# Rotary halves exchanged by ScalarE, and smaller array tiles, in the second attention of a two-layer fp32 kernel

## What is computed

```python
kv_c = kv @ W_kvc                                  # 64 compressed channels, 64 keys per batch in the kernel
q_c = q @ W_dq                                     # 96
q_nope = (q_c @ W_uq).reshape(b, lq, 16, 128);  q_rope = _rope((q_c @ W_qr).reshape(b, lq, 16, 64), lq)
k_nope, v = (kv_c @ W_uk), (kv_c @ W_uv)           # 16 heads of 128
k_rope = _rope(kv_c @ W_kr, lk)
scores = (q_nope . k_nope + q_rope . k_rope) * scale;  scores = where(good, scores, NEG)
out = softmax(scores) . v;  return out @ W_o
# _rope: x1, x2 = halves of 32;  [x1 * cos - x2 * sin, x1 * sin + x2 * cos]
# FFN: gate = silu(W_gate x), up = W_up x (704 hidden channels);  W_down (gate * up)
```

## Time and profile before

| what | us |
|---|---|
| median of 3 executions | 863.61 (861.70 to 863.77) |
| profiled execution | 862.67 |
| its span, first to last instruction | 860.87 |
| TensorE, weight loads, VectorE busy | 810.3, 692.9, 661.2 |
| ScalarE, GpSimd busy | 521.0, 457.1 |
| granted TensorE clock, mean | 0.984 |

### The profile page before, as it was taken

The page is one execution under the profiler, slowest core; times in us unless marked ns, Lnnn a source line. Parts: engine busy times, 40 slices in busy tenths (PEclk is TensorE's granted clock), DMA queues, the critical chain, the costliest instruction groups (busy, mean ns, idle before and its releaser), DMA issues.

```text
span 860.9 us, 14397 instructions
## 1 busy us (share of the span) xinstructions
PE 810.3 (94%) x4888; PEld 692.9 (80%) x4888; DVE 661.2 (77%) x1584; ACT 521.0 (61%) x1202; POOL 457.1 (53%) x776
## 2 busy tenths in 40 slices
PE   3777999999999999999899999999999999999998
PEld 2566888888888888888788788988888878777887
DVE  7988888899888998879988894955544758876534
ACT  6888877788678886788764645433322334646332
POOL 2485869779685996858953864252010028760000
PEclk9779999999999999999999999999999999999999
DMA  7000120012101030000100416947310000100001
GB/s 236 14 1 1 38 74 1 2 38 61 51 1 32 7 111 1 2 1 22 47 25 14 148 38 181 232 138 270 105 52 23 11 34 25 50 1 1 0 2 49
DMA packets 28376, 45.99 MB, mean 53 GB/s; under 512 B 3952, under 2 KB 18096, under 8 KB 28176
## 3 DMA queue, kind: packets, MB, share of 16 engines
q1 hardware_dynamic: 26800, 41.31, 16.4%
q10 hardware_dynamic: 1504, 3.77, 1.2%
HBM read 43.89 MB, written 1.18 MB: 52 GB/s over the span
## 4 chain that ended last, share of the span: by engine, by line
PE 66%; DVE 21%; ACT 9%; issue 3%; DMA 1%; SPq 0%; ACTq 0%; DVEq 0%
PE PS L760 18%; PE PS L829 8%; PE PS L716 5%; PE PS L621 5%; PE PS L652 4%; PE PS L690 4%; PE PS L930 3%; DVE cat L1498 3%; PE PS L885 2%; PE PS L662 2%; PE PS L643 2%; DVE yb L1494 2%; PE PS L673 2%; PE PS L920 2%; PE PS L700 2%
## 5 line engine op out<-in xcount | busy, mean ns | idle before, releaser
L2166 POOL TENSOR_SCALAR raw<-raw,mvq,rsq 128x128 f32<-128x128 f32 x312 | 187.6, 615 | 7.2 <-DVE mvq L1639 5.7
L760 PE MATMUL PS<-xq,WH 128*128 128x512 f32 x480 | 151.0, 396 | 0.0
L760 PEld LDWEIGHTS PS<-xq,WH 128*128 128x128 f32 x480 | 87.8, 190 | 17.0 <-issue 0.8
L760 PE MATMUL PS<-xq,WL 128*128 128x512 f32 x240 | 94.1, 392 | 0.0
L621 PE MATMUL PS<-WH,xq 128*128 128x256 f32 (+1 forms) x256 | 89.6, 367 | 3.6 <-issue 1.5
L621 PE MATMUL PS<-WL,xq 128*128 128x256 f32 (+1 forms) x256 | 84.9, 349 | 0.0
L1086 ACT ACTIVATE P<-PS,sm 128x256 f32<-128x256 f32 x128 | 60.7, 492 | 31.1 <-DVE sm L1667 30.9
L1592 DVE BATCH_NORM_STATS2 st<-raw 128x6 f32<-128x128 f32 x320 | 71.9, 276 | 0.9 <-ACT raw L1058 0.9
L829 PE MATMUL PS<-xq,m_hh 128*128 128x256 f32 x384 | 69.3, 281 | 1.4 <-DVE m_hl L1956 0.6
L716 PE MATMUL PS<-PH,cat 128*128 128x256 f32 x256 | 64.7, 292 | 6.2 <-DVE cat L1498 5.9
L690 PE MATMUL PS<-PT,vr 128*128 128x256 f32 x256 | 66.2, 381 | 1.0 <-ACT PT L972 1.0
(11 more groups left out here) (299 smaller groups left out, 2208.7 us busy)
## 6 DMA issues: line engine op xcount, KB each, us to landing
wst<-in_wgu SPq DMA_DIRECT2D x24, 256.0 KB, 3.7
l_KM<-share SPq DMA_DIRECT2D x16, 384.0 KB, 4.0
wst<-in_wall SPq DMA_DIRECT2D x18, 256.0 KB, 3.1
l_KM<-share SPq DMA_DIRECT2D x16, 256.0 KB, 4.8
dst<-in_wdn SPq DMA_DIRECT2D x24, 128.0 KB, 3.6
wst<-in_wkvx SPq DMA_DIRECT2D x8, 256.0 KB, 3.4
l_KM<-share SPq DMA_DIRECT2D x16, 128.0 KB, 4.1
m_pre<-in_wo ACTq DMA_DIRECT2D x1, 2048.0 KB, 10.1
```

Of the source, the lines that this page charges most:

```text
L760: t = e.matmul(PS[:, b, :], W[wi][:, gu, k, :], a[:, k, cols], start=(n == 0), stop=(n == 5))
L2166: t = e.tensor_scalar(v, v, mvq[:, par, n, 0:1], rsq[:, par, n:n + 1], ALU.add, ALU.mult)
```

## The change

It does the following:
- The exchanged copy of the rotary weights (wrt), its DMA and its matmuls go. One bank now holds two pairs of heads (a unit u; 4 units a batch). The columns of W_qr are reordered so that the first halves of two heads lie in partitions 0 to 63 and the second halves in 64 to 127. ScalarE copies the bank's upper half, negated, to the lower half of tqs and its lower half to the upper (`swap_q`); VectorE multiplies tqs by sin and the bank by cos; GpSimd adds. Two buffers of each go round.
- Queries come before scores in each n, and queries(1, 0) before the loop; each n from 0 to 4 has one part.
- `values2` is 8 matmuls of K = 64, M = 64 on the four quarters of the array, two fillings (of the four) at a time; BDK holds the keys on both halves in both column halves, with no zeros. `outmix` takes the heads in matching order.
- `absorb` fills both column halves, AT lies on 128 partitions, KA holds the compressed keys on both halves, and `keymix` alternates between the upper and the lower row half of the array.
- In the FFN, block 5 puts 64 channels of gate and 64 of up into one weight: one bank instead of two, and `f_down` there reads 64 rows.

```diff
-QUERIES = {0: (2, 3), 1: (4,), 2: (5,), 3: (6,), 4: (7,)}
+QUERIES = {0: (3,), 1: (4,), 2: (5,), 3: (6,), 4: (7,)}
-        if a == 0:
-            for part in range(2):
-                do("queries", 0, part)
+        for part in ((0, 0), (0, 1)) if a == 0 else ((1, 0),):
+            do("queries", *part)
     for n in range(11):
+        for m in QUERIES.get(n, ()):
+            do("queries", m // 2, m % 2)
         if n < 8:
             do("scores", n)
         if n % 2 and n > 2:
             do("values", (n - 3) // 2)
-        for m in QUERIES.get(n, ()):
-            do("queries", m // 2, m % 2)
...
-            "queries": lambda bb, part: [("qr", bb, p) for p in range(4 * part, 4 * part + 4)],
+            "queries": lambda bb, part: [("qr", bb, u) for u in range(2 * part, 2 * part + 2)],
...
 def keys():
                 for k in range(2):
-                    t = e.matmul(PS[0:64, b, 0:256], wkvc[:, k, :], ctxT[:, k, :], start=(k == 0), stop=(k == 1))
+                    for o in (0, 64):
+                        t = e.matmul(PS[o:o + 64, b, 0:256], wkvc[:, k, :], ctxT[:, k, :], start=(k == 0), stop=(k == 1))
 def absorb(z):
                 for h in range(4 * z, 4 * z + 4):
-                    t = e.matmul(PS[0:64, b, h % 4 * 96:h % 4 * 96 + 96], wuk[:, h, :], wuq[:, h, :], start=True, stop=True)
+                    o, i = 64 * (h % 2), h % 4 // 2 * 96
+                    t = e.matmul(PS[o:o + 64, b, i:i + 96], wuk[:, h, :], wuq[:, h, :], start=True, stop=True)
 def keymix():
-                for z in range(8):
-                    b = fill(("km", z))
-                    emptied(("aw", z // 2))
-                    for h in (2 * z, 2 * z + 1):
-                        t = e.matmul(PS[0:96, b, h % 2 * 256:h % 2 * 256 + 256], AT[:, h, :], KA[0:64, :], start=True, stop=True)
-                    t.then_inc(full[b], 1)
+                for y in range(4):
+                    banks = [fill(("km", 2 * y + o)) for o in range(2)]
+                    emptied(("aw", y))
+                    for i in range(2):
+                        for o, b in enumerate(banks):
+                            rows = slice(64 * o, 64 * o + 64)
+                            t = e.matmul(PS[0:96, b, i * 256:(i + 1) * 256], AT[rows, 2 * y + i, :], KA[rows, :],
+                                         start=True, stop=True)
+                            if i:
+                                t.then_inc(full[b], 1)
 def queries(bb, part):
-                for p in range(4 * part, 4 * part + 4):
-                    b = fill(("qr", bb, p))
-                    for z, W in enumerate((wqr, wrt)):
-                        t = e.matmul(PS[:, b, z * 256:(z + 1) * 256], W[:, p * 128:(p + 1) * 128],
+                for u in range(2 * part, 2 * part + 2):
+                    b = fill(("qr", bb, u))
+                    for i in range(2):
+                        p = 2 * u + i
+                        t = e.matmul(PS[:, b, i * 256:(i + 1) * 256], wqr[:, p * 128:(p + 1) * 128],
                                      qcT[:, bb * 256:(bb + 1) * 256], start=True, stop=True)
 def values2(bb):
-                for z in range(4):
-                    b = fill(("lv", bb, z))
-                    e.matmul(PS[:, b, :], BDK[:, bb, :], PT1[:, 2 * z:2 * z + 2, :].rearrange("p a b -> p (a b)"),
-                             start=True, stop=True).then_inc(full[b], 1)
+                for z in (0, 2):
+                    banks = [fill(("lv", bb, z + i)) for i in range(2)]
+                    for r, c, i in ((0, 0, 0), (64, 64, 0), (0, 64, 1), (64, 0, 1)):
+                        t = e.matmul(PS[c:c + 64, banks[i], :], BDK[r:r + 64, bb, c:c + 64],
+                                     PT1[r:r + 64, 2 * (z + i):2 * (z + i) + 2, :].rearrange("p a b -> p (a b)"),
+                                     start=True, stop=True)
+                        if r:
+                            t.then_inc(full[banks[i]], 1)
 def place_keys():
-                for o in (0, 64):
-                    copy(KZ[o:o + 64, :, o // 64, :], k23[o:o + 64]).then_inc(keys_in, 1)
+                for o in range(0, 128, 32):
+                    copy(KZ[o:o + 32, :, o // 32 % 2, :], k23[o:o + 32]).then_inc(keys_in, 1)
+            def swap_q(bb, part):
+                for u in range(2 * part, 2 * part + 2):
+                    n = 4 * bb + u
+                    b = w.filled(("qr", bb, u))
+                    if n > 1:
+                        w.wait_ge(added.sem, added.at[(n - 2) // 4, (n - 2) % 4])
+                    e.activation(tqs[u % 2][0:64, :], PS[64:128, b, :], ACT.Copy, scale=-1.0)
+                    copy(tqs[u % 2][64:128, :], PS[0:64, b, :]).then_inc(swapped.sem, 1)
 for a in (0, 2):   # ScalarE
                 take_qc(a)
                 take_qc(a + 1)
+                for part in ((0, 0), (0, 1)) if a == 0 else ((1, 0),):
+                    swap_q(*part)
             for n in range(11):   # ScalarE
+                for m in QUERIES.get(n, ()):
+                    swap_q(m // 2, m % 2)
                 if n % 2 and n > 2:
                     take_lv((n - 3) // 2)
                 if n < 8:
                     exps2(n)
 def gate_f(n):   # ScalarE; VectorE waits for gated_5 and multiplies rows 64:128 of the same bank
+                if j == 5:
+                    e.activation(fsg[n % 3][0:64, :], PS[0:64, b, :], ACT.Silu, scale=fsc[0:64, 5:6]).then_inc(gated_5.sem, 1)
+                    return
 def turn_q(bb, part):   # VectorE
-                    e.tensor_tensor(tq[n % 3], PS[:, b, :], tb_[:, 0:512], ALU.mult).then_inc(free[b], 1)
+                    if n > 1:
+                        w.wait_ge(added.sem, added.at[(n - 2) // 4, (n - 2) % 4])
+                    w.wait_ge(swapped.sem, swapped.at[bb, u])
+                    e.tensor_tensor(two[1], two[1], sin, ALU.mult)
+                    e.tensor_tensor(two[0], q, cos, ALU.mult).then_inc(free[b], 1)
 def add_q(bb, part):   # GpSimd
-                    e.tensor_tensor(QR[bb % 2][:, p, :], tq[n % 3][:, 0:256], tq[n % 3][:, 256:512],
+                    e.tensor_tensor(QR[bb % 2][:, 2 * u:2 * u + 2, :].rearrange("p a b -> p (a b)"), tqc[n % 2], tqs[n % 2],
                                     ALU.add).then_inc(added.sem, 1)
```

102 lines of the change are left out of this document (58 added, 44 removed).

## The result

The changed kernel took 872.45 us in the median of 8 runs (867.47 to 874.99), the kernel before 863.69 (860.54 to 865.45) beside it: ratio 1.0098, 95% interval 1.0068 to 1.0127. The forecast was 859.3, range 855.0 to 863.5: wrong in sign and outside the range. The profiled execution took 869.8 us, with a span of 868.0 against 860.87.

A forecast was written before the change was run, and what follows sets the result against it. TensorE was taken as the bound, balanced in the loop by a VectorE and ScalarE ring. Terms -1.1, +0.5, +0.9, 0, -1.5, -1.4, -0.75 gave -3.35 us on 862.67: 859.3 us, range 855 to 863.5.

The forecast's parts named there:

- TensorE loses 3.5 us per chunk and has room: Loop: fewer query matmuls take 3.5 us per chunk off TensorE; the pitch was not expected to follow.
- the ring's: Loop: VectorE and ScalarE set the pitch, 9.8 us between starts of soft(n)'s row maxima (M_n); M_0 to M_7 unchanged.
- GpSimd's sums stand ahead of the weights of that n: Loop: GpSimd adds the rotary products before converting that n's weights; VectorE and ScalarE keep the 9.8 us pitch.
- The wait at n = 3: Chunk 3's exponentials wait 4.7 us more for values(0)'s banks and copies; M_3 to M_4 takes 14.7 us.
- The opening: From keymix to the first row maximum: two-buffer ring of swap, products and GpSimd sum; maximum at 710.4 us, +0.9.
- Rival D: Opening: GpSimd's 512-column additions could take 2.2 us beside VectorE; first maximum 2 us later, 861.3 us; chance 0.15.
- Before the late stage: Ahead of keymix: absorbing keys in pairs -1.1 us, placing rotary keys with four copies +0.5 us, the rest nothing.
- Keymix: Two row tiles take 3.7 us instead of 7.14; copies through four banks let x2T copies start 2.35 us earlier.
- Tail: After the loop: values(3) -1.5 us, FFN block j = 5 at h = 0 -1.4, last down group -0.75.
- A: Values: array tiles run only in program order, 3.9 us a call; total 862.0 us; chance 0.12.
- C: Values: four tiles run one after another, 6.9 us a call; total 871.9 us; chance 0.05.
- B: Chunk 3: the new wait does not bind or is short, M_4 4.7 us earlier; total 854.6 us; chance 0.1.

The follow-up runs named there:

- e1: Changed kernel with idle matmuls into an unused bank ahead of compress(2), the queries of n = 0 to 3 and inside values(0): 868.12 us, ratio 1.0051.
- e15: The kernel of e9 with idle matmuls ahead of compress(2), queries(2, 1) and (3, 0), and inside values(0): 863.58 us, ratio 0.9986.
- e9: Changed kernel with values(0)'s copies behind chunk 3's exponentials, three rotary buffers, and GpSimd's last three weight pieces held until xn_f(0): 866.54 us, ratio 1.0049.
- e12: The kernel of e9 with TensorE's order back to scores, values, queries, and GpSimd's weight conversions behind the scaling of soft(n): 867.38 us, ratio 1.0040.
- e13: Kernel before with all edits but the rotary one, GpSimd's conversions behind the scaling, last three pieces held: 857.10 us, ratio 0.9926; run again 858.37, 0.9946.
- e16: The kernel of e15 with GpSimd's weight conversions behind the scaling of soft(n): 859.75 us, ratio 0.9956.
- e4: Changed kernel with GpSimd holding the last three FFN weight pieces (6, 7, 8) until add_l(0) is done: 868.84 us, ratio 1.0066.
- e5: Changed kernel with ScalarE's copies of values(0) put behind chunk 3's exponentials instead of ahead: 869.85 us, ratio 1.0090.
- e14: Changed kernel without ScalarE's exchange across partitions, sine products reading the bank directly, queries not rotated rightly: 865.08 us, ratio 1.0015.

## Why the prediction was wrong, point by point

**"TensorE is full in nearly all of it, at a granted clock of 1.00, which leaves the clock out of this case."** This is the step that failed first. A clock that is full because the engine is full says nothing of a change that takes work off this engine. With "TensorE loses 3.5 us per chunk and has room" I wrote down the idle time and priced it at nothing. The runs: 872.45 to 868.12 for filling the gaps (e1), and 1.0049 to 0.9986 where the other waits were mended (e15 against e9). It is not the largest term. Of the 10.5 us between the forecast and the profiled execution, by the points below, about 3.9 are matmuls at half clock, 4.4 VectorE's operations beside GpSimd's, 1.0 the start, 0.6 the late copies of l_x2T and 0.6 the tail.

**"So the pitches from M_0, M_1, M_2 and M_4 are the ring's: 9.8 each."** They were 10.4, 12.2, 10.8 and 9.9. Of the 4.0 us over the forecast from M_0 to M_3, 0.6 a chunk, 1.8, is the scaling, 2.3 us long where it was 1.65 to 1.7: GpSimd's conversions stand beside it. The forecast took 9.8 from a row that already had part of the stretch in it; without GpSimd beside it the pitch is 9.3 (e12, e13, e16). The other 2.2 is queries and scores at half clock: with the fillers of e1 all three are 10.4, and they are near it, too, in e4's execution, where hardly more than the queries ran slow.

**"GpSimd's sums stand ahead of the weights of that n"**: right, but what it delays was not followed up. The last three pieces now lie on add_l(0), whose steps of 0.16 us take 1.1 beside them. M_5 to M_7 took 23.6 and not 21.0 us: 2.6 of the 6.7. In e4 these two pitches are 20.6 together; M_4 to M_5 takes 1.2 of the gain back.

**The wait at n = 3: right in place and size, wrong in what it is worth.** M_3 to M_4 took 14.8 us, the forecast was 14.7 (the 3.4 us that it gives for TensorE at n = 4 should be 3.6, 13.4 less 9.8; no term hangs on it). But taking it away on ScalarE's side (e5) gave 1.5 us and no ratio that differs. TensorE's own chain through the same bank is only 1.5 us shorter. No order that I tried brought this pitch under 12.9 with the rotary edit.

**The opening: mechanism right, size off.** Forecast +0.9, measured +3.1. Rival D's cause, a slower sum (1.44 us in the mean and not 1.27), and exchanges of 1.22 us a unit, where 1.1 was taken, delay the copies of l_x2T by 0.6 us, counted from the start of keymix. The larger part, 1.7, is the clock again: compress(2, 3) 3.27 instead of 1.94, the sixteen query records behind it 4.01 instead of 3.6. Three buffers and the clock kept bring the opening to 25.1 (e9, e15); without the exchange, in the same order, it is 22.5 (e14).

**Before the late stage.** absorb gave 0.65 us for two calls, 1.3 in all (forecast 1.1); place_keys took 1.72 us for 0.84, +0.9 (forecast +0.5, bound +0.85). The start of keymix is 0.4 us later and not 0.6 earlier; since variants of the changed kernel that are the same up to there start keymix anywhere from 684.34 to 689.54, no run here can settle this.

**Keymix: right.** From keymix's start to the copies of x2T 5.4 us, forecast 5.5; the second half of it waited 0.39 us for a copy, as the bank argument said.

**Tail: right, but for the FFN.** values(3) gave 1.5, as forecast; block 5 for h = 0 gives 1.0 where 1.4 was forecast; the last down group begins 0.7 us sooner after f_front(5, 1) than before (4.36 to 3.65; forecast 0.75), TensorE waiting 0.81 us for Silu, product and copy as foreseen, but its 18 records then take 2.58 us and not 2.39. The rows show one cause for both: where matmuls of 64 rows follow such of 128, or the other way round, the next record starts some 0.1 us late and the first pair lasts 0.1 longer, 0.2 a change, with two changes at h = 0 and one at the end. The forecast had counted 0.2 for such changes in values and left them out here.

**The rivals.** A and C are refuted by a values call of 1.95 us; the one of 3.51 is not their case but the clock's. B, that the wait at n = 3 doesn't bind, is false in the rows and nearly true in worth. C's time, 871.9, was near the result, for a reason that had nothing to do with it: the slower side had a chance of 0.12 and no rival with the cause that decided. The one that was missing is TensorE at half clock in the idle time that the change itself makes.

**A rule that was weighed.** The values rows show 16 records of 512 columns in 1.95 us, four at a time. By the rule of strict order in the Trainium skill (TensorE: Matmul & The Clock Gate, Part 3), read so that the second pass of each fp32 matmul holds up the next tile, a call would have taken 3.9 us, an estimate from these rows. The trace does not agree with that reading.

## What to carry to other kernels

Work taken off the busiest engine does not only leave it idle: ask what its granted clock will be then, and price the matmuls behind each new gap at the lower level as well. In a ring of buffers between engines that go in order, one wait usually lies in the shadow of another; price a wait by what is next late when it is gone, and test mends in pairs. Before more work goes to GpSimd or less to TensorE, look at which operations of VectorE, short ones too, it will then stand beside.

## What was not expected of the hardware

- Idle matmuls made the program faster: 872.45 to 868.12 us, and 1.0049 to 0.9986 on top of other mends.
- Half clock came after gaps of 4.17 and 2.96 us but not after another of 2.97, and a `project` call behind 1.27 us of idle time ran slow in one execution and not in the other of the same program. Behind the same gap in the same program compress(2, 3) took 3.27, 2.87 and 3.51 us (changed kernel, e4, e5). Runs of the changed kernel scatter more (867.5 to 875.0) than those of the kernel before (860.5 to 865.5).
- Copies of ScalarE from partitions 64 to 127 to 0 to 63 and back take 0.59 us and follow each other at 0.61: they didn't overlap, where copies of 128 partitions take 1.08 for two.
- A step of VectorE of 0.16 us takes 1.1 beside GpSimd, a scaling of 1.23 takes 2.33, and GpSimd's own 0.61 becomes 1.59.
- Four array tiles of 64 rows and 64 columns run at once, with fp32's two records a matmul: 16 records of 512 columns in 1.95 us.
